# Local attention: scores and sums of V as 64-row matmuls of alternating row halves

## The reference

```
w = 32                                   # window
bk2, bv2 = look(bk), look(bv)            # window before and own window: 64 keys
sim = einsum('bhwie,bhwje->bhwij', bq, bk2) * 8.0      # 32 queries x 64 keys, over 64 features
attn = softmax(where(mask, -max, sim))
out = einsum('bhwij,bhwje->bhwie', attn, bv2)          # 32 queries x 64 features, over 64 keys
return out.transpose(0, 2, 1, 3).reshape(b, n, 1024) @ Wo
```

## Time and profile before

| | |
|---|---|
| time, median of 3 runs | 5635.59 us (5633.15 to 5646.27) |
| the profiled execution: its own time, its span | 5633.29 us, 5631.3 us |
| mean granted clock of TensorE | 0.903 |
| PE matmul busy | 4707.3 us, 84% |
| DVE busy | 3589.5 us, 64% |
| ACT busy | 2466.6 us, 44% |
| POOL busy | 2512.1 us, 45% |

### The profile page before, as it was taken

The page is one execution under the profiler, slowest core; times in us unless marked ns, Lnnn a source line. Parts: engine busy times, 40 slices in busy tenths (PEclk is TensorE's granted clock), DMA queues, the critical chain, the costliest instruction groups (busy, mean ns, idle before and its releaser), DMA issues. The chain is left out here.

```text
span 5631.3 us, 144287 instructions
## 1 busy us (share of the span) xinstructions
PE 4707.3 (84%) x58081; PEld 3028.4 (54%) x58081; DVE 3589.5 (64%) x6107; ACT 2466.6 (44%) x3020; POOL 2512.1 (45%) x3540
## 2 busy tenths in 40 slices
PE   3555567776779998899988999799988999889997
PEld 2333322222236666566655666466665666556664
DVE  6665556655646666566756666566666666656675
ACT  2433433443344444444534444344443444434453
POOL 1000011111146664566626666266654666356671
PEclk9888877887789999999999999999999999989999
DMA  0000000000012221222212222122221222122220
GB/s 27 0 0 0 0 1 0 0 0 0 0 47 71 68 67 47 54 67 67 68 30 71 67 67 65 36 67 67 70 61 38 69 71 67 39 54 70 72 66 22
DMA packets 156765, 246.36 MB, mean 44 GB/s; under 512 B 33488, under 2 KB 50896, under 8 KB 155472
## 3 DMA queue, kind: packets, MB, share of 16 engines
q1 hardware_dynamic: 156240, 238.09, 15.9%
HBM read 20.38 MB, written 2.10 MB: 4 GB/s over the span
## 5 line engine op out<-in xcount | busy, mean ns | idle before, releaser
L1151 DVE TENSOR_TENSOR ls_a<-PS,TC 128x1024 f32<-128x1024 f32 x384 | 467.6, 1219 | 424.4 <-ACT ls_r L1079 424.4
L1074 ACT ACTIVATE ls_q<-ls_q 128x512 f32<-128x512 f32 x384 | 242.0, 630 | 891.1 <-DVE ls_q L1170 891.1
L1161 DVE TENSOR_REDUCE ls_ss<-ls_r 128x16 f32<-128x1024 f32 x384 | 466.2, 1214 | 256.6 <-ACT ls_r L1094 256.6
L1156 DVE TENSOR_TENSOR ls_q<-PS,TS 128x512 f32<-128x512 f32 x768 | 491.1, 680 | 19.5 <-POOL ls_a L881 19.5
L948 PE MATMUL PS<-ls_kT,ls_qT 64*32 64x64 f32 x24576 | 483.0, 233 | 6.8 <-issue 6.7
L948 PEld LDWEIGHTS PS<-ls_kT,ls_qT 64*32 64x32 f32 x24576 | 411.4, 117 | 121.3 <-issue 121.1
L381 POOL TENSOR_TENSOR QT<-MXT,ONE 3x512 bf16<-3x512 bf16 x128 | 146.9, 1148 | 729.6 <-ACT MXT L534 722.4
L961 PE MATMUL PS<-WQ,ls_xsT 128*128 128x512 f32 x768 | 453.1, 720 | 16.6 <-issue 15.3
L872 POOL TENSOR_TENSOR ls_nw<-ls_ss,ls_nw 128x32 f32<-128x32 f32 x192 | 48.3, 252 | 925.0 <-DVE ls_rn L1200 925.0
L881 POOL TENSOR_TENSOR ls_a<-ls_a,ls_q 128x1024 f32<-128x1024 f32 x192 | 451.9, 2354 | 15.0
L884 POOL TENSOR_TENSOR ls_a<-ls_a,ls_q 128x1024 f32<-128x1024 f32 x192 | 453.3, 2361 | 0.0
(11 more groups left out here) (215 smaller groups left out, 9400.6 us busy)
## 6 DMA issues: line engine op xcount, KB each, us to landing
ls_vb<-ls_vt SPq DMA_DIRECT2D x1152, 130.0 KB, 2.4
ls_vb<-ls_vt SPq DMA_DIRECT2D x672, 65.0 KB, 2.0
ls_xs<-XL SPq DMA_DIRECT2D x42, 256.0 KB, 4.0
WQ<-wqkv SPq DMA_DIRECT2D x6, 1536.0 KB, 6.6
ls_vb<-ls_vz SPq DMA_DIRECT2D x96, 65.0 KB
WO<-wo SPq DMA_DIRECT2D x24, 128.0 KB, 6.3
X<-x SPq DMA_DIRECT2D x8, 256.0 KB, 4.5
out<-X SPq DMA_DIRECT2D x8, 256.0 KB, 3.5
```

What stands on the lines that cost most here:

```text
L1151: nc.vector.tensor_tensor(v4(A[fq])[:, a], src, tab, ALU.mult).then_inc(done, 1)
L1156: ins = nc.vector.tensor_tensor(v4(SW)[:, a, :, lo:lo + h2], src[:, :, hi:hi + h2], TS[:, ft, a, lo:lo + h2].unsqueeze(1).to_broadcast([P, ...
L1161: nc.vector.tensor_reduce(ss[:, fq, a * H:a * H + H], v4(SQ)[:, a], AX.X, ALU.add).then_inc(done, 1)
```

## The change

Three things are changed in the attention of the 6 layers. The scores are made for a pair of heads at a time, four windows of the head in the first row half and then four of the one in the second; both banks get their masks first. The sums of V are made for one head at a time over its own 64 rows, 65 columns, again the two row halves in turn; the block of zeros in `VB` is gone (its memset, L840, has half the columns). The sums of heads in the first row half go to bank 5, of the others to bank 6, and the last pair's to banks 4 and 7. DVE's reciprocals and products take the new places. `s_po` is raised by PE and nobody waits for it.

```diff
-            VB = two("ls_vb", [P, NW, 2, H // 2, DH + 1])
+            VB = two("ls_vb", [P, NW, H // 2, DH + 1])
...
-            S_BANK, PT_BANK, O_BANK, W_BANK, X_BANK = (7, 5), (7, 4), 5, 0, 1
+            S_BANK, PT_BANK, O_BANK, O_LAST, W_BANK, X_BANK = (7, 5), (7, 4), (5, 6), (4, 7), 0, 1
...
                             for a in range(2):
-                                o = banks(S_BANK[a])
-                                pe.matmul(o, identb[:, :], winb[:, 0 if t else 1, :].unsqueeze(1).to_broadcast([P, H // 2, 2 * WIN]),
+                                pe.matmul(banks(S_BANK[a]), identb[:, :], winb[:, 0 if t else 1, :].unsqueeze(1).to_broadcast([P, H // 2, 2 * WIN]),
                                           start=True, stop=False)
-                                r = slice(a * DH, a * DH + DH)
-                                for i in range(H // 2):
+                            for i in range(H // 2):
+                                for a in range(2):
+                                    r = slice(a * DH, a * DH + DH)
                                     for w in range(NW):
                                         k0 = t * P + WIN * w
-                                        ins = pe.matmul(o[WIN * w:WIN * w + WIN, i * 2 * WIN:(i + 1) * 2 * WIN], qT[r, i, WIN * w:WIN * w + WIN],
-                                                        kT[r, i, k0:k0 + 2 * WIN], start=False, stop=(i == H // 2 - 1))
-                                ins.then_inc(s_so, 1)
+                                        ins = pe.matmul(banks(S_BANK[a])[WIN * w:WIN * w + WIN, i * 2 * WIN:(i + 1) * 2 * WIN],
+                                                        qT[r, i, WIN * w:WIN * w + WIN], kT[r, i, k0:k0 + 2 * WIN],
+                                                        start=False, stop=(i == H // 2 - 1))
+                                    if i == H // 2 - 1:
+                                        ins.then_inc(s_so, 1)
...
                             for i in range(H // 2):
-                                for w in range(NW):
-                                    at = (i % 3) * 2 * (DH + 1)
-                                    ins = pe.matmul(banks(O_BANK + i // 3)[WIN * w:WIN * w + WIN, at:at + 2 * (DH + 1)],
-                                                    PRT[:, i * P + WIN * w:i * P + WIN * w + WIN], VB[q][:, w, :, i, :], start=True, stop=True)
+                                for e in range(2):
+                                    r = slice(e * DH, e * DH + DH)
+                                    o, at = (banks(O_BANK[e]), i * (DH + 1)) if i < H // 2 - 1 else (banks(O_LAST[e]), 0)
+                                    for w in range(NW):
+                                        ins = pe.matmul(o[WIN * w:WIN * w + WIN, at:at + DH + 1], PRT[r, i * P + WIN * w:i * P + WIN * w + WIN],
+                                                        VB[q][r, w, i, :], start=True, stop=True)
```

More of the change, by code:

```diff
@@ L732, in program @@
             s_vb = sems("v_windows")
-            s_vo = sem("windows_open")
+            s_vo, s_po = sem("windows_open"), sem("values_open")
             s_ak, s_aq, s_bk, s_bq = sem("k_cos"), sem("q_cos"), sem("k_sin"), sem("q_sin")
@@ L814, in slot @@
                                 before = VT[1 - q][P - WIN:P, e] if t else VZ[:, :, :]
-                                sp.dma_start(VB[q][at:at + WIN, 0, e], before).then_inc(s_vb[q], 16)
-                                sp.dma_start(VB[q][at + WIN:at + DH, 0, e], VT[q][0:WIN, e]).then_inc(s_vb[q], 16)
+                                sp.dma_start(VB[q][at:at + WIN, 0], before).then_inc(s_vb[q], 16)
+                                sp.dma_start(VB[q][at + WIN:at + DH, 0], VT[q][0:WIN, e]).then_inc(s_vb[q], 16)
                                 for w in range(1, NW):
-                                    sp.dma_start(VB[q][at:at + DH, w, e], VT[q][WIN * (w - 1):WIN * (w + 1), e]).then_inc(s_vb[q], 16)
+                                    sp.dma_start(VB[q][at:at + DH, w], VT[q][WIN * (w - 1):WIN * (w + 1), e]).then_inc(s_vb[q], 16)
                     def stage(b):
@@ L839, in _ @@
                     pool.memset(VT[s][:, :, :, :], 1.0).then_inc(s_zero, 1)
-                    pool.memset(VB[s][:, :, :, :, :], 0.0).then_inc(s_zero, 1)
+                    pool.memset(VB[s][:, :, :, :], 0.0).then_inc(s_zero, 1)
                 pool.memset(ss[:, 0, B + 2:B + 3], 0.0).then_inc(s_res, 1)
@@ L979, in slot @@
                             pe.wait_ge(s_vb[q], windows(l, b, t))
+                            pe.sem_inc(s_po, 1)
                             for i in range(H // 2):
[L981 to L984 removed]
+                                for e in range(2):
[4 more added lines that the diff above has]
+                                                        VB[q][r, w, i, :], start=True, stop=True)
                             ins.then_inc(s_o, 1)
@@ L1181, in slot @@
                             dve.wait_ge(s_o, n)
[L1182 to L1187, removed]
+                            most = PS[:, O_BANK[0]:O_BANK[1] + 1, 0:(H // 2 - 1) * (DH + 1)].rearrange("p e (i d) -> p e i d", d=DH + 1)
+                            last = PS[:, O_LAST[0]:O_LAST[1] + 1:O_LAST[1] - O_LAST[0], 0:DH + 1]
+                            r2 = rc[:, :].rearrange("p (e i) -> p e i", e=2)
+                            y2 = Y.rearrange("p (i e d) -> p e i d", e=2, d=DH)
+                            wide = lambda z, k: z.unsqueeze(3).to_broadcast([P, 2, k, DH])
+                            nc.vector.reciprocal(r2[:, :, 0:H // 2 - 1], most[:, :, :, DH])
+                            nc.vector.reciprocal(r2[:, :, H // 2 - 1], last[:, :, DH]).then_inc(s_rc, 1)
                             dve.wait_ge(s_rc, n)
-                            nc.vector.tensor_tensor(y6, full[:, :, :, 0:DH], r6.unsqueeze(3).to_broadcast([P, 2, 6, DH]), ALU.mult)
-                            nc.vector.tensor_tensor(Y[:, 12 * DH:].rearrange("p (h e) -> p h e", e=DH), rest[:, :, 0:DH],
-                                                    rc[:, 12:H].unsqueeze(2).to_broadcast([P, 4, DH]), ALU.mult).then_inc(s_y, 1)
+                            nc.vector.tensor_tensor(y2[:, :, 0:H // 2 - 1], most[:, :, :, 0:DH], wide(r2[:, :, 0:H // 2 - 1], H // 2 - 1), ALU.mult)
+                            nc.vector.tensor_tensor(y2[:, :, H // 2 - 1], last[:, :, 0:DH], r2[:, :, H // 2 - 1].unsqueeze(2).to_broadcast([P, 2, DH]),
+                                                    ALU.mult).then_inc(s_y, 1)
                         if front:
```

## The result

The changed kernel takes 5838.64 us (median of 4 runs, 5828.44 to 5842.96) where the kernel before takes 5634.37 (4 runs, 5625.54 to 5646.27). The ratio is 1.0352, 95% interval 1.0327 to 1.0378. The forecast was 5535 us, faster: sign and size are both wrong. The profiled execution took 5828.44 us, 195.2 more than that of before, at the same mean clock, 0.903.

The account below looks back on a forecast made before the run. A DVE and ACT chain was taken to bound ordinary slots, PE only first and last ones. Terms -82 - 18 - 10 - 2 + 8 = -104, kept as -98, took 5633.3 us to 5535; range 5505 to 5650.

Parts of the forecast that it names:

- Gain 0: Ordinary slots: sums of V end 0.9 us sooner, but nobody wants them before DVE is ready, so nothing is gained.
- between 0 and +0.1: Ordinary slots: the cost in us of bank 7's later signal, taken as 0; each 0.1 would cost 10 us in all.
- D: Rival: part of the first slots' time is not PE's, such as a longer jump; half the gain, 5585 us, chance 0.08.
- I take 7: Scores and sums of V: 7 ns a row, full overlap of the row halves; no overlap would be 14.
- just hidden: Ordinary slots: first bank's scores ready 1.66 us from the start, just when DVE comes to the maxima; cost 0.
- +8 us for third slots: Third slot of a pass: maxima start at 1.66 us instead of 1.47, +0.19 us, 42 times.
- A: Rival: row halves overlap only in part, shown by 10 ns a row; sum +8, 5641 us, chance 0.14.
- B: Rival: row halves do not overlap, 14 ns a row, first bank ready at 2.5 us; +117, 5750 us, chance 0.12.
- at 10.4 the gain is gone: Scores past 1.66 us from the slot's start cost time; at 10.4 ns a row nothing of the gain is left.
- forecast -82 and -10 for the clock: First slots: ACT's squares start 1.95 us sooner in 42 slots, -82 us; ten first slots at full clock, another -10.
- forecast -18: Last two slots of a layer: shorter sums of V at the low clock, -3 us a layer, -18 in all.
- rival C: The lower clock spreads through PE's idle gaps in ordinary slots; +112 us if in all 102, near 5640, chance 0.06.

Follow-up runs that it names:

- e3: The kernel before with only the new sums of V, all heads of the first row half, then all of the second: 5839.51 us, ratio 1.0374.
- e5: The whole change plus 64 semaphore increments once in PE's program, ahead of the loop over the layers: 5680.3 us, ratio 1.0074 to the kernel before.
- e8: The whole change with 130 columns instead of 65 in each matmul of the sums of V, not the reference's sums: 5890.96 us (one run).
- e1: The kernel before with only the scores as changed, the sums of V as before: 5672.43 us, ratio 1.0066.
- e7: The kernel before with the new scores in the first slot of each loop pass alone: 5612.7 us, ratio 0.9962.
- e10: The kernel before with new scores in each pass's first slot alone, plus 172 semaphore increments at PE's start: 5637.3 us, ratio 0.9991.
- e2: The kernel before with only the sums of V as changed, the scores as before: 5829.78 us, ratio 1.0351.
- e11: The kernel before with only 172 semaphore increments added at PE's start: 5685.03 us, ratio 1.0085.
- e4: The whole change plus 64 semaphore increments on PE in each layer, ahead of its slots: 5750.74 us (one run).

## Why the prediction was wrong, and where it was right

**What failed, first in size: the count of instructions.** The section on the change says of the sums of V "Twice as many matmuls of half the columns"; the prediction counts their time in the array ("0.9 for 1.75") and puts "Gain 0" for an ordinary slot, with "between 0 and +0.1" for the later signal as all that could be lost. The price of 128 more instructions a burst is put at nothing, without a reason; it never asks how a burst of 256 instructions comes to PE. Measured are 90 stalls, 165.7 us, and +184.0 us in the slots that have them. Three bursts a pass now run out of instructions, one behind the jump, which did so briefly before, and two in the sums of V. What the runs show of the mechanism: a burst of sums of V stands behind a wait (for the transposed exponentials). If it begins in the first 44 instructions of a block, it uses up the block within 1.3 to 1.9 us; the packet of the next block starts only after that wait has ended, and PE goes on 2.8 to 3.9 us after the burst's start (3.1 to 3.7 in after), at whatever pace the rows went (e3). If it begins at 66 or later, the packet of the next block has moved before the wait's end (e5). e5 against after prices the placement alone, with every instruction of the loops kept: 158 us of the 204 that separate the medians of after and before. Of the rivals none names it. D speaks of a longer jump: the jump stayed (83.0 to 74.4 us).

**Second: "I take 7".** The price of a row is 9.9 ns. The bounds of 7 and 14 held it, and the overlap of the row halves that it was to stand for is complete (e8). What else holds the rows at 9.9, the supply at two instructions a row as it seems, was not among the limits that I weighed. The text says "10 ns is A": by its own sign the prediction would have taken this for a partial overlap, and e8 says it is none. The hold-up that A describes, of one half by the other's second round, would have given 20 ns a row in e8, where 14.1 were measured.

**Third: the later signal of the first bank.** Forecast at 1.66 us from the slot's start, "just hidden". It is 3912.64 - 3910.66 = 1.98, and DVE waits 0.22 us, where in the earlier trace rows it doesn't wait. In the third slots it is 2.00 in the mean, where it was 1.47. The prediction's own sum gives this when the price is put right: 0.53 + 120 x 0.0099 + 0.27 = 1.99. So this step follows from the second one. The term was +8 us for third slots and 0 for the others. e1 and e5, where these slots have no stalls, give +41.6 and +42.6 for second and third slots together, 0.5 us each. That is what A and B charge for, and the prediction had said of it that "at 10.4 the gain is gone". In e1 and e5, where the sums of V do not stall, it eats the first slots' gain (48.5 and 31.8 us).

**Fourth: the first slots, forecast -82 and -10 for the clock.** They gave -45.2 (13.6 and 31.6). The part behind the stall is right in kind: less work of PE at the lower clock, and the time at that clock in a first slot of a pass went from 7.39 to 4.92 us in the mean. But 46.2 us went to the stall in L948 behind the jump (1.28 each): 172 instructions behind the jump the block is at its end, and PE at its new pace gets there before the next has come. That -92 and +46 meet at the -45 measured is in part luck, since the rows were slower than forecast: e7 has the same stall and gives -32, and e10, at another placement, has 35.5 us of stalls there and gives -81.

**Fifth: a layer's last slots, forecast -18.** They cost instead: +15.4 in the 30th, +8.1 in the 31st and +19.4 in the last with the feed-forward. The 30th has one of the stalls. In the 31st the time at the lower clock doubled, from 4.55 to 9.10 us. The way from the last slot to the feed-forward was 24.1 us in 4 layers and 27.7 in 2; it is 27.8 to 28.1 in all, at the lower clock. This looks like rival C, the spreading of the lower clock, in a place where it wasn't put. It was not tested by a run of its own: e5, without the stalls, still loses 9.0 and 10.9 there, e1 2.9 and 19.7.

**What held.** DVE and ACT bound the ordinary slots: e2's third slots stay at 15.61 us with sums of V 0.5 us shorter. DVE's new shapes cost nothing: 1.09 + 0.28 us is the forecast's 1.37. The mean clock did not fall (0.903). The place where PE is waited for is the pass's first slot, and the new scores made there alone are the fastest kernel of all (e7).

**What stays open.** By what rule a block is asked for: for sums of V the place lies between 44 and 66 instructions into the block ahead of it (63 goes either way), but for scores 32 is enough, so a fixed place alone does not explain it. What holds a row at 9.9 ns. Why the lower clock spreads at the layer's end, and why it lasts longer in e7's first slots than in e1's. And no placement was found where the whole change has no stall at all; its best is e5, 0.7% above before, and by the third point it could gain only what the first slots give less some 42 us.

## What to carry to other kernels

Count instructions beside array time: matmuls cut in two may cost nothing in the array and still be paid in their supply, as stalls where a burst as long as a block stands behind a wait, and it seems as a slower pace (here 10 ns a row). An "issue" wait in the middle of a burst is the sign; count PE's instructions between two such waits, and if they are whole blocks apart, move the code by a few dozen empty instructions before judging the change, since placement alone was worth 158 us here. And shorten an engine only where it is waited for: the new scores were worth -0.4% in one slot of four and nothing or less in the other three.

## What the runs showed of the hardware that I had not expected

- Eight tiles of 64 by 32 of the array work side by side without loss in f32: 14.1 ns a row at 130 columns (e8), where one row alone would take 110, an estimate from the 112 ns of a row of 128 columns in the earlier trace rows.
- Behind the first 32 rows of a burst, a weight load and a matmul of 64 columns together take 10.6 ns, some 5 ns an instruction (scores of after).
- The packet that brings PE 256 instructions can start as late as after the wait ahead of a burst that needs it. PE goes on 1.2 to 1.6 us after the packet's end, so a straight stretch of program without any branch can stall by up to 2.3 us (longest wait at L988).
- Where the code lies within its blocks is worth more than the change was meant to bring: 158 us between after and e5, and in e11, with the loops of before untouched, -42 us in the first slots and +65 in the second and third.
- An increment of a semaphore by PE that does nothing else cost 74.2/172 = 0.43 us at the program's start and up to 89.0/(6 x 64) = 0.23 us in e4.
